# Moving the second norm of sequences 1 to 6 among the first instructions of a transformer kernel's layers

## The reference

```python
x = x + _L0_attn_ref(_layernorm(x, axis=-1), L0_attn_Wq, ..., L0_attn_g_norm_weight)
x = x + _L0_ffn_ref(_layernorm(x, axis=-1), L0_ffn_Wqkv, ..., L0_ffn_b2)
```

```python
x = attn_layer(shift_tokens(x), Wqkv[i], q_scale[i], k_scale[i], Wo[i]) + x
x = ffn_layer(shift_tokens(x), ln_g[i], ln_b[i], W1[i], b1[i], W2[i], b2[i]) + x
```

## Time and profile before

| | |
|---|---|
| median of three runs | 4912.56 us (4911.16 to 4913.23) |
| the profiled execution, own time | 4920.57 us |
| its span, first to last instruction | 4918.5 us |
| PE busy | 4697.9 us (96%) |
| POOL, DVE, ACT busy | 3860.9 (78%), 3709.6 (75%), 3167.2 us (64%) |
| mean granted clock of PE | 0.981 of full |
| the layers begin | near 1716 us |

### The profile page before, as it was taken

How to read it: one execution, slowest core, us unless ns; L and a number is a source line. 1 busy time by engine, 2 the same in 40 slices (tenths; PEclk the granted TensorE clock), 3 DMA queues, 4 the chain that set the end, 5 groups by cost and what they waited for, 6 DMA issues and landing times.

```text
span 4918.5 us, 226955 instructions
## 1 busy us (share of the span) xinstructions
PE 4697.9 (96%) x99180; PEld 3434.8 (70%) x99180; DVE 3709.6 (75%) x5109; ACT 3167.2 (64%) x4833; POOL 3860.9 (78%) x3744
## 2 busy tenths in 40 slices
PE   5999999999999869999999999999999999999997
PEld 3788888888888636666666666666666666666664
DVE  3677777777777468788787888878878887888884
ACT  3677777777777446666666666666666666666664
POOL 2677777777777488788888888888888888888883
PEclk6999999999999989999999999999999999999999
DMA  1000000000000102322232222322232223222222
GB/s 51 3 4 4 8 4 4 4 8 4 4 8 4 34 23 65 90 64 65 69 86 67 69 69 66 82 64 69 69 82 69 66 65 90 69 66 79 66 73 61
DMA packets 154831, 238.83 MB, mean 49 GB/s; under 512 B 42746, under 2 KB 53368, under 8 KB 152952
## 3 DMA queue, kind: packets, MB, share of 16 engines
q1 hardware_dynamic: 153848, 224.32, 17.4%
HBM read 24.96 MB, written 4.19 MB: 6 GB/s over the span
## 4 chain that ended last, share of the span: by engine, by line
PE 89%; DVE 3%; issue 3%; POOL 2%; ACT 1%; DVEq 0%; POOLq 0%; ACTq 0%
PE banks L170 74%; PE banks L174 15%; DVE arena L1213 1%; DVE arena L1197 1%; DVE arena L1248 0%; POOL arena L2397 0%; ACT arena L1008 0%; DVE arena L2252 0%; POOL arena L2358 0%; POOL arena L2367 0%; DVE arena L1256 0%; POOL arena L1448 0%; ACT arena L953 0%; DVE arena L1238 0%; ACT arena L1991 0%
## 5 line engine op out<-in xcount | busy, mean ns | idle before, releaser
L170 PE MATMUL banks<-arena 64*32 64x64 f32 (+7 forms) x92652 | 4017.9, 248 | 159.5 <-issue 42.6
L170 PEld LDWEIGHTS banks<-arena 64*64 64x64 f32 (+3 forms) x92652 | 2725.9, 132 | 1190.2 <-issue 803.8
L174 PE MATMUL banks<-arena 128*128 128x128 f32 x6528 | 894.6, 278 | 57.9 <-POOL arena L2397 32.2
L2367 POOL TENSOR_TENSOR arena<-arena 128x1024 f32<-128x1024 f32 x384 | 910.3, 2371 | 41.8 <-DVE arena L2193 41.6
L174 PEld LDWEIGHTS banks<-arena 128*128 128x128 f32 x6528 | 735.9, 141 | 289.4 <-issue 241.9
L2397 POOL TENSOR_TENSOR arena<-arena 128x1024 f32<-128x1024 f32 x384 | 728.0, 1911 | 11.4
L2184 DVE TENSOR_TENSOR arena<-banks,arena 128x1024 f32<-128x1024 f32 x384 | 468.1, 1219 | 103.1 <-ACT arena L1991 99.2
L2193 DVE TENSOR_TENSOR arena<-banks,arena 128x512 f32<-128x512 f32 x768 | 490.8, 680 | 1.1 <-POOL arena L2367 1.1
L1197 DVE SCALAR_TENSOR_TENSOR arena<-banks,arena 128x256 f32<-128x256 f32 x768 | 368.8, 480 | 152.2 <-ACT arena L962 115.5
L1448 POOL TENSOR_TENSOR arena<-arena 128x256 f32<-128x256 f32 x384 | 334.5, 875 | 189.1 <-DVE arena L1197 187.9
L2404 POOL TENSOR_TENSOR arena<-arena 128x1024 f32<-128x1024 f32 x192 | 368.0, 1917 | 140.7 <-DVE arena L2232 140.7
(11 more groups left out here) (133 smaller groups left out, 4759.8 us busy)
## 6 DMA issues: line engine op xcount, KB each, us to landing
arena<-arena SPq DMA_DIRECT2D x1152, 128.0 KB
arena<-arena SPq DMA_DIRECT2D x672, 64.0 KB
arena<-in_Wqkv SPq DMA_DIRECT2D x6, 1536.0 KB, 7.2
arena<-in_Wo SPq DMA_DIRECT2D x6, 512.0 KB
outT<-arena SPq DMA_DIRECT2D x4, 512.0 KB, 3.0
arena<-outT SPq DMA_DIRECT2D x8, 256.0 KB, 4.7
outT<-arena SPq DMA_DIRECT2D x8, 256.0 KB, 2.7
arena<-in_W SPq DMA_DIRECT2D x6, 341.0 KB
```

The lines of the kernel that those rows point to most:

```text
L170: return e.matmul(o, lhsT, rhs, start=start, stop=stop, skip_group_check=True)
L174: return e.transpose(o, i, mat["ident"][0:n, 0:n])
L2367: e.tensor_tensor(T1, T1, T2[i], ALU.add).then_inc(sg(f"g_rope{i}"), 1)
```

## The change

Nothing is added or removed. Steps of the second norm stand at other places of the four lists:

- PE: the two matmuls `late_mean` 3 and 4 stand behind `project_rows` (0,1,0) instead of in front of it.
- ACT: `log_sum` and `root` of block (0,0) stand ahead of the late steps of sequences 3 and 4, instead of behind them.
- DVE: `late_make_dve` 4 stands ahead of the cosines and sines of block 2 of pass 0, instead of between the two sums of that block.
- POOL: `late_make_pool` 1 and 2 stand behind `floor_sums` of block 0 and of block 1 of pass 0, one each, instead of both behind `normalise` of block 1; `late_make_pool` 3 stands behind `floor_sums` of block 2 instead of behind its `normalise`.

```diff
@@ layers_pe
                 if n == 0:
                     late_centre(e, 3)
                     late_centre(e, 4)
-                    late_mean(e, 3)
-                    late_mean(e, 4)
...
                 project_rows(e, n, 1, 0, [("a_turned0", n - 1, 3), ("v_sin0", n, 0)])
                 if n == 0:
+                    late_mean(e, 3)
+                    late_mean(e, 4)
                     late_centre(e, 5)
                     late_centre(e, 6)
                     late_mean(e, 5)
@@ layers_act
                 square_rows(e, n - 6, 1, 1)
+                copy_q(e, n - 7, 3)
+                log_sum(e, n - 6, 0)
+                copy_y(e, n - 8, 3)
+                root(e, n - 6, 0)
                 if n == 6:
                     late_square(e, 3)
                     late_square(e, 4)
...
                     late_root(e, 3)
                     late_root(e, 4)
-                copy_q(e, n - 7, 3)
-                log_sum(e, n - 6, 0)
-                copy_y(e, n - 8, 3)
-                root(e, n - 6, 0)
                 square_rows(e, n - 6, 1, 0)
@@ layers_dve
                 sum_squares(e, n, 1, 1)
                 sum_squares(e, n, 1, 0)
+                if n == 0:
+                    late_make_dve(e, 4)
                 refine(e, n - 2)
...
                 sum_squares(e, n, 2, 1)
-                if n == 0:
-                    late_make_dve(e, 4)
                 sum_squares(e, n, 2, 0)
@@ layers_pool
                 normalise(e, n - 3, 1, 1)
                 normalise(e, n - 3, 1, 0)
-                if n == 3:
-                    late_make_pool(e, 1)
-                    late_make_pool(e, 2)
                 add_rope(e, n - 3, 2, 1)
                 floor_sums(e, n - 3, 2)
+                if n == 3:
+                    late_make_pool(e, 3)
                 add_rope(e, n - 3, 2, 0)
...
                 normalise(e, n - 3, 2, 0)
-                if n == 3:
-                    late_make_pool(e, 3)
                 add_rope(e, n - 3, 3, 1)
...
                 floor_sums(e, n - 2, 0)
+                if n == 2:
+                    late_make_pool(e, 1)
                 refine_root(e, n - 2, 0)
...
                 floor_sums(e, n - 2, 1)
+                if n == 2:
+                    late_make_pool(e, 2)
                 add_rope(e, n - 2, 1, 1)
```

## The result

| | before | change |
|---|---|---|
| first measurement, median | 4913.23 us (9 runs) | 4903.34 us (9 runs) |
| ratio, 95% interval | | 0.9976 (0.9967 to 0.9986) |
| second measurement, another chip, median | 4916.25 us (27 runs) | 4908.47 us (11 runs) |
| ratio, 95% interval | | 0.9986 (0.9978 to 0.9995) |
| profiled execution, own time | 4920.57 us | 4907.36 us |

The account below looks back on a forecast made before the run. POOL was taken as what every engine waits for, up to DVE's sine of (1,0,1). Filled gaps of 7.39 and 3.10 us, less contention, give 9.4; less 1.1 at PE, 8.3 saved: 4904.3 us, range 4901 to 4907.

Parts of the forecast that it names:

- Late block 1 in the gap of 7.39 us at 7.07: POOL, after its first floor_sums: the block costs 7.07 us and fills the idle gap of 7.39 us almost exactly.
- The price of 8.70: POOL's upper price per late block, beside DVE's late blocks; for late block 1 it would save 1.3 us less.
- ACT's and PE's moves at nothing: Earlier root of block 0 on ACT and earlier project_rows (0,1,0) on PE: zero by themselves, PE at most 0.5 us.
- DVE's late block 4, 7.5 us, hidden: DVE, in its gap of 7.12 us: the block takes 7.5 us, costing block 2's cosine 0.4 us, which is hidden.
- Late block 2 at 8.70, block 3 at 8.70: POOL, beside DVE's late blocks: each costs 8.70 us; block 2 fills the 3.10 us gap, block 3 cost 7.07 before.
- POOL's chain: POOL's steps from its first floor_sums to add_rope (0,3,1), which starts at 1780.7 instead of 1790.12: 9.4 us gained.
- New wait of DVE of 4.8 us, no consequence: DVE's sine (0,2,1) waits 4.8 us for POOL's add_rope (0,1,1); DVE's later sums still finish just in time.
- PE last before ACT's square of (1,0,1), cosine at 56.0: PE's transposes and matmuls end last, so cosine (1,0,1) comes at 1786.0 instead of 1794.41; 1.1 us of POOL's gain lost.
- Late block 6 beside POOL, 6.9 us (6.8 before and the 0.1 added): DVE, between cosine (1,0,1) and the sine freeing the key banks: beside POOL as before, 0.1 us added to 10.35.
- What lies behind the meeting point repeats itself: After DVE's sine of (1,0,1), where all four engines meet, everything repeats, only shifted; 8.3 us earlier there is the saving.
- Rival B: PE costs nothing: POOL's 9.4 us pass whole and the slow stretch behind 1804.82 shortens, 4903 to 4899.5 us; chance 0.27.
- Rival C: Gain mostly lost to dearer late blocks beside DVE and to PE's clock: 3.3 us saved, 4909 us; chance 0.15.
- Rival D: DVE takes POOL's place through its new wait and dearer late blocks: 8.9 us slower, near 4921.5 us; chance 0.06.

Follow-up runs that it names:

- experiment 2: The change without its ACT and PE moves, POOL and DVE as in the change: 4908.70 us, ratio 0.9983 to the kernel before.
- experiment 1: The change without its DVE move, late_make_dve 4 again between the two sums of block 2: 4910.78 us, ratio 0.9991 to the kernel before.
- the second profile: The change itself, unaltered, run and profiled once more on another chip: 4908.47 us, ratio 0.9986 to the kernel before.
- experiment 7: The change with late_make_dve 7 moved later on DVE, behind the reciprocal of (0,3): 4903.17 us, ratio 0.9977 to the kernel before.
- experiment 6: The change with late_make_dve 6 one place earlier, in front of the cosine of (1,0,1): 4905.14 us, ratio 0.9984 to the kernel before.
- experiment 4: The kernel before with a single move, late_make_pool 1 behind floor_sums of block (0,0): 4911.47 us, ratio 0.9990 to the kernel before.
- 5: The change with late_make_pool 3 back behind normalise of block 2: 4906.75 us, ratio 0.9980 to the kernel before.
- experiment 10: The change with late_make_pool 3 moved behind subtract (0,0), into POOL's wait: 4905.62 us, ratio 0.9982 to the kernel before.
- experiment 9: The change with late_make_pool 3 a pass later, in front of normalise_p (0,3): 4903.40 us, ratio 0.9976 to the kernel before.

## Why the prediction was right

The forecast was 4904.3 us, 8.3 below before; 9.9 and 7.8 us were measured, and D fell by 9.1. The times alone could not have told 8.3 from 6 or 11; it is the steps in the trace that bear the forecast out. Step by step, times counted from the end of the first `floor_sums`:

- *Late block 1 in the gap of 7.39 us at 7.07:* 7.12 measured, start to start. DVE ran one cosine and two sines with one operand in PSUM beside it, and neither the block nor they were slower (L2184 took 1.22 us there as elsewhere). The Trainium skill ("SBUF — State Buffer", section "Who interferes with whom") states that a DVE instruction with at most one SBUF input does not contend with GpSimd, outside the 2-port modes; the prediction left this condition out, and by the same section `tensor_tensor` instructions, as these are, have no such mode. The trace agrees, 7.12 us. The price of 8.70 would have cost 1.6 us more here, not the 1.3 that the prediction states.
- *ACT's and PE's moves at nothing:* 0.2 us (experiment 2), within the spread of D.
- *DVE's late block 4, 7.5 us, hidden:* 7.1 us, hidden. Its place matters by 2.6 us (experiment 1); the prediction priced only the place that was chosen.
- *Late block 2 at 8.70, block 3 at 8.70:* 8.53 and 8.55. With the instructions around them, rounding included, POOL's chain came out 0.8 us shorter than the sum: its `add_rope` (0,3,1) started at 49.9 instead of 50.7 (before: 60.1), so POOL gained 10.2 us and not 9.4. This is the term that was mis-sized.
- *New wait of DVE of 4.8 us, no consequence:* 4.55, none at the end.
- *PE last before ACT's square of (1,0,1), cosine at 56.0:* 55.4 (55.1 in the second profile). PE was the last there, as forecast: ACT's square waited 0.78 us for it (the row under experiment 7) and started 2.5 us after the four matmuls did, 1782.62 against 1780.10, where 2.4 was taken. POOL's gain of 10.2 us was 9.0 at the cosine, so 1.2 us was lost, forecast 1.0. That the four matmuls came at 2.5 is in part luck: with the same order they took 1.9 in experiment 7, at full clock.
- *Late block 6 beside POOL, 6.9 us (6.8 before and the 0.1 added):* 6.6. It gave back 0.2 us where 0.1 was to be lost.
- *What lies behind the meeting point repeats itself:* M fell by 9.4 and 9.8 where D fell by 9.1, so nothing was lost. The prediction's reason, that all four engines meet there, holds for this change, and experiment 6 shows where it ends: with D 4.5 us smaller POOL had no slack left, a longer wait of PE with a fall of its clock came behind, and the gain was nearly gone by M.

*Rival B* did not come: 1.2 us was lost on the way to the cosine, and the slow stretch behind the meeting point was nearly as long as before, transposes 1.97 and matmuls 3.78 in both, and the next transposes 1.64 against 1.91. *Rival C* did not come; the prices beside DVE were below, not above, those taken. *Rival D*, DVE in POOL's place, did not come in the change, but its mechanism is real: in experiments 4, 5 and 10 PE's transposes of block 2 wait for DVE's sine behind late block 5. In 4 and 5 this bounds nothing, since ACT's `log_sum` of block 3 then waits 5.42 and 5.09 us for POOL. In experiment 10, where POOL is quicker, it does: the cosine came 3 us later than D = 58 asked for.

The profiled spans differ by 13.0 us, more than D explains. 1.8 us of it lie before the first `floor_sums`, 9.1 in D, 0.3 between D and M, and 1.8 behind M; these last were not traced to a cause.

## What to carry to other kernels

Look for the event at which every engine waits for the same instruction: up to it, one engine's list can be added up row by row. Behind it a shift passed through here as long as the engine with the most work still had an idle gap at that event; where it had none (experiment 6), the gain was lost to it and to a longer wait of PE with a lower clock behind. Fill an engine's gaps with work that is due later before anything else is moved: here one block in one gap of the right length was most of the gain of six moves. Where a kernel's runs spread by more than the effect, compare distances between two events in the traces, take the second event well behind the last move, and profile one order more than once to learn the spread of the distance itself.

## What the hardware showed that was not expected

- Where DVE's L537, with two SBUF inputs, met one long instruction of POOL (four places compared, in before, the change and experiment 4), it ended 0.54 to 0.56 us after POOL's did, so the price depends on the neighbour's size: L537 took 0.69 us alone, 1.59 beside POOL's 128x512 (before, 1755.87), 2.02 behind the rest of a 128x1024 (the change, 1741.29), and 2.75 behind nearly the whole of one in experiment 4. POOL's instructions wait in the same way, the small ones too (L2383: 0.25 us alone, 0.70 in experiment 4). The same five DVE instructions cost 5.7 us (experiment 1) to 8.4 us (late block 7 in experiment 9) by what stood beside them.
- The slow stretches of PE's clock do not always fall on the same instructions from profile to profile. The four matmuls at 1737.69 in the change (`late_mean` 5 and 6, behind a wait of 3.3 us) took 3.78 us in six of the eleven traces with this order of PE, 3.41 in one and 2.10 in four. With the old order, behind a wait of 2.1 us, they took 2.10 in all three. At the meeting point such a difference moved D by 0.7 us without any cause in the order (experiment 7 against the change).
